# Attention row maxima read 512 keys at a time through four one-bank slots, with the attention stage written out group by group

## The chip, the core and the metric

The kernel runs on one core of one Trainium2 chip. The metric is the device time of one execution in microseconds (us). The kernel before takes 3453.68 us (median of 3 runs, 3448.55 to 3458.07).

## The reference, cut to what matters

Eight sequences of 1024 rows with 512 features go through a layer normalisation, an attention with 16 heads of 32 features (queries and keys come from low-rank projections and partly carry a rotary embedding), a residual sum, a second normalisation and a gated feed-forward part. The change touches only the attention:

```python
query = qt_c + qt_r
key = kt_c + kt_r
attn = jnp.einsum('bhqd,bhkd->bhqk', query, key) / scale
attn = jax.nn.softmax(attn, axis=-1)
out = jnp.einsum('bhqk,bhkd->bhqd', attn, value)
```

The softmax needs, for each of the 1024 queries of each head, the largest of its 1024 products with the keys.

## The kernel before, in words

The program has four stages, one behind the other: fold_block combines the projection weights, project_block normalises x and computes queries, keys and values, attend_block is the attention, and mix_block is everything behind it. The projection and the mixing stage are loops of the engines (Fori) with their first and last pieces written out.

The attention works on 32 groups (NG), each of one sequence and four heads. For one group PE computes two things:

- **The maxima of the group that comes next** (max_product, L242 to L261). A tile is 128 queries of one head against all 1024 keys. It takes two products of 512 keys each (the two values of kc), which go into the two banks of one slot. There are 2 slots of 2 banks (ps_m, MR = 2). VectorE (DVE) reads a whole slot, 1024 columns, with one reduce_max (max_reduce, L264 to L276), and writes one column of row_max. 16 tiles make a half of a group (HALF_TILES), and a group has two halves. Behind each half PE transposes the 16 columns of row_max in one of the same slots (L253), DVE turns the sign (L272, neg_max), and a transfer puts the result into one row of the query stack (stack_max, L279 to L284). PE may write a slot when DVE has read it (semaphore m_read, L249).
- **The attention of this group** (scores L797 to L806, pv L808 to L819, sums L821 to L831). A group has 8 rounds (UNITS). A round is 8 score products (512 queries against 128 keys of one head, the maximum subtracted through the extra row of the stacks), 8 exponentials on ScalarE (ACT, L893) out of a ring of three banks (ps_s), 16 narrow products that sum probabilities times values into ps_o (L818), and on GpSimd (POOL) one sum of the probabilities in pairs (L912; one more, L916, per half). Twice per group, 24 narrow products (L829) sum the pairs.

The order on PE is a hand-written table. SPREAD says how many steps of the maxima go ahead of each score product: one ahead of each of the 8 of a round. So a round on PE alternates maximum product, score product, eight times, and then come the 16 narrow products of the round before. Two places differ. In the fifth round two steps go ahead of the third score; the first of the two is the transpose for half 0. And the last step of a group, behind the narrow products of its eighth round, is the transpose for half 1. STEPS is 66 per group: 64 products and 2 transposes. Group 0 has a table of its own, SPREAD_FIRST, with nothing in its first two rounds and 11 steps in most of the others. The maxima of group 0 itself are computed in the last part of project_block, 5 or 6 steps for each projection item, in the PSUM tensors ps_turned and ps_rotated; DVE's part of it is at L641 to L652.

The attention stage is run through rounds(eng, step) (L735): groups 0 to 2 written out, then an engine loop over i = 1 to 9 with three groups in its body (27 groups), then groups 30 and 31 written out. In the loop, PE, DVE and the others take the values they wait for from registers. Names used below: "maximum product" is L258, "score product" L805, "the narrow products" L818.

Of the kernel before, what the change touches and what calls it, by code (L numbers as in the profile page):

```python
# [31 lines left out]
HG = P // HD  # L32
NG = B * FC
CH = 512
# [8 lines left out]
def is_first(c):  # L43

    return type(c) is int and c == 0


def fold_block(nc, sem, t, w, att, drams, load_x):
# [3 lines left out]
    with ExitStack() as ctx:  # L52
# [153 lines left out]
R3 = 3  # L206
NQ = S // CH
QT = CH // P
ROWS = 3 * HD
MR = 2  # L210
HALF_TILES = HG * QT


USE = ([(0, j) for j in range(HALF_TILES)] + [(1, 0), (0, HALF_TILES)] +
       [(1, j) for j in range(1, HALF_TILES + 1)])
USES = len(USE)
ROWS_AT = [USE.index((half, HALF_TILES)) for half in range(2)]
LAST_TILE_AT = [USE.index((half, HALF_TILES - 1)) for half in range(2)]
STEP = [(u, kc) for u, (half, j) in enumerate(USE) for kc in range(1 if j == HALF_TILES else S // CH)]
STEPS = len(STEP)  # L220
LOADS = 3 * NQ + 3


# [16 lines left out]
    sp.dma_start(att["v"][r][:], v_d[n]).then_inc(att["v_loaded"][r], 16)  # L240


def max_product(nc, pe, att, slots, ident, m, r, loads, step):


    u, kc = STEP[step]
    half, j = USE[u]
    slot = slots[u % MR]
    if kc == 0 and (u >= MR or not is_first(m)):  # L249
        pe.wait_ge(att["m_read"], m * USES + u - MR + 1)  # L250
    if j == HALF_TILES:
        pe.wait_ge(att["m_read"], m * USES + LAST_TILE_AT[half] + 1)
        nc.tensor.transpose(slot[0:HALF_TILES, 0, 0:P], att["row_max"][:, half, :], ident[:]).then_inc(att["m_scored"], 1)  # L253
        return
    if step == 0:
        pe.wait_ge(att["loaded"][r], 16 * LOADS * loads)
    h, q = divmod(j, QT)
    product = nc.tensor.matmul(slot[:, kc, :], att["q"][r][0:ROWS, half, h, q * P:(q + 1) * P],  # L258
                               att["k"][r][0:ROWS, h, kc * CH:(kc + 1) * CH], start=True, stop=True)
    if kc == S // CH - 1:  # L260
        product.then_inc(att["m_scored"], 1)  # L261


def max_reduce(nc, dve, att, slots, m, u):  # L264

    half, j = USE[u]
    slot = slots[u % MR]
    dve.wait_ge(att["m_scored"], m * USES + u + 1)
    if j == HALF_TILES:
        if not is_first(m):  # L270
            dve.wait_ge(att["m_stacked"][half], 16 * m)
        nc.vector.tensor_scalar(att["neg_max"][:, half, :], slot[0:HALF_TILES, 0, 0:P], -1.0, None,  # L272
                                ALU.mult).then_inc(att["m_read"], 1)
        return
    nc.vector.reduce_max(att["row_max"][:, half, j:j + 1], slot[:, :, :].rearrange("p k t -> p (k t)"),  # L275
                         AX).then_inc(att["m_read"], 1)  # L276


def stack_max(sp, held, att, n, r, half):  # L279
# [7 lines left out]
def project_block(nc, sem, held, t, w, x_v, x_in, x_loaded, att, grouped, scratch):  # L287
# [18 lines left out]
    with ExitStack() as ctx:  # L306
# [18 lines left out]
        rotated_too = ctx.enter_context(nc.psum_tensor("ps_rotated", [P, 2, CH], F32))  # L325
        ps_t = [turned[:, i, :] for i in range(TR)]
        ps_r = rotated_too[:, 0, :]
        ps_m = [turned, rotated_too]
        ps_p = [ctx.enter_context(nc.psum_tensor(f"ps_p{i}", [P, CH], F32)) for i in range(RING)]

        ln_step = sem("ln_step")
# [229 lines left out]
        def _(dve):  # L561
# [67 lines left out]
            def body(i, last):  # L629
                for par in range(CPB):  # L630
                    c = i * CPB + par
                    more = not (last and par == CPB - 1)
                    dve.wait_ge(rot_y, c + 1)
                    if not is_first(c):
                        dve.wait_ge(rot_sum, c * 2)
                    dve.sem_inc(held, 1)
                    nc.vector.stream_shuffle(y_swap[:, :], y_rot[:, :], SWAP).then_inc(rot_swap, 1)  # L637
                    if more:
                        norm(c + 1, 1 - par, i + 1 + par)
                    if last and par == CPB - 1:  # L640

                        for n in range(NI):
                            begun = ENDS[n - 1] if n else 0
                            uses = [u for u, kc in STEP[begun:ENDS[n]] if USE[u][1] == HALF_TILES or kc == 1]
# [22 lines left out]
def attend_block(nc, sem, held, t, att, scratch, o_d, l_d):  # L667
# [6 lines left out]
    UNITS = NQ * ROUNDS  # L674
    UT = KB * HG
    TILES = UNITS * UT
    SR = 3
    PR = 3
# [4 lines left out]
    RUN = TILES + NQ  # L683
    L_AT = UT
    HALF_RUN = ROUNDS * UT + 1
    assert RUN % SR == 0 and R3 * UNITS % PR == 0 and USES % MR == 0

    def is_last(n):
        return type(n) is int and n == NG - 1
# [15 lines left out]
    with ExitStack() as ctx:  # L705
# [9 lines left out]
        o_sb = sb("o_sb", [P, NQ, CH])  # L715
        l_sb = sb("l_sb", [P, NQ, CH])
        ps_s = [ctx.enter_context(nc.psum_tensor(f"ps_s{i}", [P, CH], F32)) for i in range(SR)]
        ps_m = [ctx.enter_context(nc.psum_tensor(f"ps_m{i}", [P, S // CH, CH], F32)) for i in range(MR)]
        ps_o = ctx.enter_context(nc.psum_tensor("ps_o", [P, CH], F32))

        rows_set = sem("rows_set")
# [10 lines left out]
        LOOPS = NG // R3  # L732
        REST = NG - LOOPS * R3

        def rounds(eng, step):  # L735

            for r in range(R3):
                step(0, r, r)
            with eng.Fori(1, LOOPS) as i:
                for r in range(R3):  # L740
                    step(i, r, i * R3 + r)
            for r in range(REST):
                step(LOOPS, r, LOOPS * R3 + r)

        @block.sync
        def _(sp):
            def store_o(n, qc):
                sp.wait_ge(o_out, n * NQ + qc + 1)
                sp.sem_inc(held, 1)
                sp.dma_start(o_d[n, :, qc * CH:(qc + 1) * CH], o_sb[:, qc, :]).then_inc(o_stored[qc], 16)  # L750

            def store_l(n, qc):
                sp.wait_ge(exped, taken(n, l_place(n, qc)))
                sp.sem_inc(held, 1)
                sp.dma_start(l_d[n, :, qc * CH:(qc + 1) * CH], l_sb[0:P - HD + 1:HD, qc, :]).then_inc(l_stored[qc], 16)

            def step(i, r, n):
# [19 lines left out]
            rounds(sp, step)  # L777
# [16 lines left out]
        def _(pe):  # L794
# [64 lines left out]
                    sums(n, 1)  # L859

            pe.wait_ge(att["ones_done"], 1)
            rounds(pe, step)

        @block.scalar
        def _(act):
# [30 lines left out]
                    take_o(n, 1)  # L896
                    take_l(n, 1)

            rounds(act, step)

        @block.gpsimd
        def _(pool):
# [16 lines left out]
            rounds(pool, step)  # L919

        @block.vector
        def _(dve):
            def step(i, r, n):
                if not is_last(n):
                    for u in range(USES):
                        max_reduce(nc, dve, att, ps_m, n + 1, u)

            rounds(dve, step)


def mix_block(nc, sem, held, t, x_d, o_d, l_d, inv_d, wo_d, wr_d, wk_d, wv_d, bo_d, mur_d, muk_d, out_d):
# [455 lines left out]
def block_program(nc, x, wdqT, bdq, wuq, buq, wqr, bqr, wkr, bkr, wdkvT, bdkv, wuk, buk, wuv, buv, wo, bo,  # L1387
# [10 lines left out]
    with ExitStack() as ctx:  # L1398
        def sem(name):
            return ctx.enter_context(nc.semaphore(name))  # L1400
# [8 lines left out]
        def keep(name, shape, dt=F32):  # L1409
            return kept.enter_context(nc.sbuf_tensor(name, shape, dt))  # L1410
# [2 lines left out]
            "q": [], "k": [], "v": [],  # L1413
            "ones": keep("ones", [P, HD]),
            "ones_done": sem("ones_done"),
            "row_max": keep("row_max", [P, 2, HG * QT]),
# [4 lines left out]
            "m_read": sem("m_read"),  # L1421
            "m_stacked": [sem(f"m_stacked{h}") for h in range(2)],
        }
        group_buffers(att, keep, 0)
# [73 lines left out]
```

## Time and profile before

| what | value |
|---|---|
| median of 3 runs | 3453.68 us (3448.55 to 3458.07) |
| the profiled execution's own time | 3445.66 us |
| its span, first to last instruction | 3443.9 us |
| PE busy | 3220.4 us, 94% |
| DVE busy | 2139.1 us, 62% |
| ACT busy | 1539.5 us, 45% |
| POOL busy | 2029.1 us, 59% |
| mean granted clock of PE | 0.975 |

The profile is of one execution. Busy shares are means over four stages that have different limits. The attention stage lies between about 686 and 2583 us of the span. PE's busy share counts matmuls whose ends are modelled and which overlap; how PE moves is read better from the starts in the timeline. A wait named "issue" is one for which the profile shows no releaser.

### The profile page before, as it was taken

To read this page: it belongs to the slowest core of one execution; us is meant where nothing else is said; L and a number is where in the kernel's file an instruction comes from. 1 tells how busy PE (TensorE), PEld (TensorE's weight loads), DVE (VectorE), ACT (ScalarE), POOL (GpSimd) and SP (SyncE) were. 2 spreads that over 40 slices of the span, in tenths; PEclk is the share of its full clock that TensorE was granted. 3 is DMA by queue.
4 is the path that set the end of the run, shared out by engine and by line. 5 is a ranking of instruction groups with operands and counts; after the bars stand their busy time and mean duration, and the time that the engine had idled before them with its cause. 6 is when DMAs were issued, how large, how long until landed. Compare 5 with 4: busy or idle time off the path is not lost. (4 is left out here: it accounts for less than half of the span.)

```text
span 3443.9 us, 49569 instructions
## 1 busy us (share of the span) xinstructions
PE 3220.4 (94%) x16020; PEld 2032.6 (59%) x16020; DVE 2139.1 (62%) x2249; ACT 1539.5 (45%) x2714; POOL 2029.1 (59%) x654
## 2 busy tenths in 40 slices
PE   7999999989999999999999999999995999999998
PEld 4888888744444444444444444444434777777777
DVE  4445545756666666666666666666617777777774
ACT  1212212156665666565666665666652322232232
POOL 0112112057777777777777777777773656556653
PEclk9999999989999999999999999999996999999999
DMA  3554545453232324242323223232205133233220
GB/s 103 176 170 160 183 167 174 141 109 79 68 82 57 93 51 96 54 96 54 88 62 77 73 67 82 57 90 53 53 13 173 50 98 97 60 86 97 81 65 37
DMA packets 179891, 316.27 MB, mean 92 GB/s; under 512 B 16081, under 2 KB 52081, under 8 KB 179697
## 3 DMA queue, kind: packets, MB, share of 16 engines
q1 hardware_dynamic: 179696, 313.70, 33.0%
q8 instruction: 120, 1.97, 0.2%
q14 instruction: 75, 0.61, 0.1%
HBM read 194.59 MB, written 118.49 MB: 91 GB/s over the span
## 5 line engine op out<-in xcount | busy, mean ns | idle before, releaser
L275 DVE TENSOR_REDUCE row_max<-ps_m 128x1 f32<-128x1024 f32 x992 | 1156.6, 1221 | 631.2 <-PE ps_m L258 630.6
L912 POOL TENSOR_TENSOR pairs<-probs 128x2048 f32<-128x2048 f32 x256 | 1167.9, 4574 | 477.2 <-ACT probs L893 477.2
L893 ACT ACTIVATE probs<-ps_s 128x512 f32<-128x512 f32 x2048 | 1085.9, 599 | 536.6 <-PE ps_s L805 520.3
L258 PE MATMUL ps_m<-k_stack,q_stack 96*128 96x512 f32 x1984 | 868.6, 439 | 97.3 <-DVE row_max L275 46.2
L805 PE MATMUL ps_s<-q_stack,k_stack 97*128 97x512 f32 x2048 | 823.4, 405 | 6.2 <-PEq L306 4.1
L258 PEld LDWEIGHTS ps_m<-k_stack,q_stack 96*128 96x128 f32 x1984 | 378.5, 191 | 532.8 <-DVE row_max L275 391.7
L818 PE MATMUL ps_o<-probs,v_tiles 128*32 128x512 f32 x4096 | 495.7, 602 | 0.0
L805 PEld LDWEIGHTS ps_s<-q_stack,k_stack 97*128 97x128 f32 x2048 | 394.7, 193 | 87.6 <-ACT probs L893 21.7
L541 POOL TENSOR_TENSOR y_cos<-y_rot,cos 64x512 f32<-64x512 f32 x16 | 20.6, 1284 | 472.8 <-DVE y_swap L637 472.8
L916 POOL TENSOR_TENSOR pairs<-pairs 128x2048 f32<-128x2048 f32 x64 | 293.2, 4581 | 5.0
L818 PEld LDWEIGHTS ps_o<-probs,v_tiles 128*32 128x32 f32 x4096 | 107.4, 109 | 248.6 <-issue 191.3
L1273 POOL TENSOR_TENSOR gate<-gate,xs 128x512 f32<-128x512 f32 x64 | 113.1, 1770 | 117.0 <-DVE gate L1363 117.0
L829 PE MATMUL ps_s<-pairs,ones 128*32 128x512 f32 x1536 | 177.6, 595 | 3.0 <-POOL pairs L912 3.0
L1091 PE MATMUL mix_p<-mix_w_o_hi,o_hi 128*128 128x512 f32 x256 | 110.8, 433 | 73.3 <-DVE gate L1363 34.9
L1195 ACT ACTIVATE relu<-mix_p 128x512 f32<-128x512 f32 x64 | 38.3, 598 | 308.1 <-PE mix_p L1093 253.1
L1352 DVE TENSOR_TENSOR ka_lo<-relu,ka_hi 128x512 fp32r<-128x512 f32 x64 | 117.3, 1833 | 49.0 <-ACT ka_hi L1189 46.7
L1244 POOL TENSOR_TENSOR xs<-mix_x_in,bo 128x512 f32<-128x512 f32 x64 | 114.7, 1796 | 25.6 <-DMA mix_x_in<-in_x 21.2
L829 PEld LDWEIGHTS ps_s<-pairs,ones 128*32 128x32 f32 x1536 | 49.8, 110 | 118.6 <-issue 113.8
L1331 DVE SCALAR_TENSOR_TENSOR mixed<-diff,mu_k,xT 128x512 f32<-128x512 f32 x64 | 111.4, 1799 | 0.6
L1092 PE MATMUL mix_p<-mix_w_o_lo,o_hi 128*128 128x512 f32 x256 | 109.4, 427 | 0.0
L1262 POOL TENSOR_TENSOR relu<-relu 128x512 f32<-128x512 f32 x64 | 68.8, 1084 | 68.8 <-ACT relu L1195 67.5
L1093 PE MATMUL mix_p<-mix_w_o_hi,o_lo 128*128 128x512 f32 x256 | 109.1, 426 | 0.0
(174 smaller groups left out, 4679.1 us busy)
## 6 DMA issues: line engine op xcount, KB each, us to landing
q_stack<-q_hi_scratch SPq DMA_DIRECT2D x128, 256.0 KB, 6.1
k_stack<-k_hi_scratch SPq DMA_DIRECT2D x64, 512.0 KB, 10.8
x_in<-in_x SPq DMA_DIRECT2D x16, 1024.0 KB, 5.7
q_hi_scratch<-st_hi SPq DMA_DIRECT2D x64, 256.0 KB, 2.3
q_lo_scratch<-st_lo SPq DMA_DIRECT2D x64, 256.0 KB, 2.6
k_hi_scratch<-st_hi SPq DMA_DIRECT2D x64, 256.0 KB, 2.4
k_lo_scratch<-st_lo SPq DMA_DIRECT2D x64, 256.0 KB, 2.7
v_scratch<-st_v SPq DMA_DIRECT2D x64, 256.0 KB, 2.3
```

The costliest lines, as they stand in the source:

```text
L258: product = nc.tensor.matmul(slot[:, kc, :], att["q"][r][0:ROWS, half, h, q * P:(q + 1) * P], att["k"][r][0:ROWS, h, kc * CH:(kc + 1) * CH ...
L275: nc.vector.reduce_max(att["row_max"][:, half, j:j + 1], slot[:, :, :].rearrange("p k t -> p (k t)"), AX).then_inc(att["m_read"], 1)
L805: nc.tensor.matmul(ps_s[v % SR][:, :], ks[r][:, a, kt * P:(kt + 1) * P], qs[r][:, qc, a, :], start=True, stop=True).then_inc(scored, 1)
L818: m = nc.tensor.matmul(ps_o[a * HD:(a + 1) * HD, :], vt[r][:, kt, a * HD:(a + 1) * HD], probs[:, (r * UNITS + u) % PR, k, a, :], start=kt ...
L829: m = nc.tensor.matmul(ps_s[v % SR][a * HD:(a + 1) * HD, :], ones[:, :], pairs[:, w, a, :], start=k == 0, stop=k == SUMS - 1)
L893: nc.scalar.activation(probs[:, (r * UNITS + u) % PR, x // HG, x % HG, :], ps_s[place(u * UT + x) % SR][:, :], ACT.Exp, scale=SCALE).then_ ...
L912: nc.gpsimd.tensor_tensor(pairs[:, w, :, :], probs[:, (r * UNITS + u) % PR, 0, :, :], probs[:, (r * UNITS + u) % PR, 1, :, :], ALU.add).th ...
L916: nc.gpsimd.tensor_tensor(pairs[:, 1, :, :], pairs[:, 0, :, :], pairs[:, 1, :, :], ALU.add).then_inc(pair_done, 1)
L1244: nc.gpsimd.tensor_tensor(xs[par][:, s, :], x_in[:, s, :], bo[:, :], ALU.add).then_inc(xb_done, 1)
L1273: nc.gpsimd.tensor_tensor(gate[:, s, :], gate[:, s, :], xs[par][:, s, :], ALU.add).then_inc(out_done, 1)
L1331: v = nc.vector.scalar_tensor_tensor(mixed[:, f, :], diff[:, f, :], mu_k[:, f:f + 1], prev[:, f, :], ALU.mult, ALU.add)
L1352: nc.vector.tensor_tensor(ka_lo[:, g, :], relu[:, g % RELU, :], ka_hi[:, g, :], ALU.subtract).then_inc(kal_done, 1)
```

## The change

- A slot is now one bank, and there are four (MR = 4; ps_m is four tensors of [128, 512], in project_block the four banks of ps_turned and ps_rotated).
- Each product of 512 keys is a use of its own: PE waits for its bank ahead of each product and signals behind each, and DVE reads each with a reduce_max of 512 columns. The result goes into part_max, two columns per tile.
- Behind the last reduction of a half, DVE waits for its own reads and takes the maximum of the two halves of part_max, 128 x 16, into row_max (new semaphore m_rows). The transpose waits for that.
- The transposes do not count in the rotation of the banks (BANK): a transpose uses the bank of the product that follows it, and that product waits until the transpose has been read (EARLIER).
- rounds() writes out all 32 groups; there is no engine loop in the attention stage, and all values that are waited for are constants.

The number of products, scores, exponentials, additions and transfers stays. DVE's reductions per group go from 32 of 1024 columns to 64 of 512, and 2 small maxima are added.

```diff
-MR = 2
+MR = 4
...
+def tiles(half, first, last):
+    return [(half, j, kc) for j in range(first, last) for kc in range(KCS)]
+
+
+USE = tiles(0, 0, HALF_TILES) + tiles(1, 0, 1) + [(0, HALF_TILES, 0)] + tiles(1, 1, HALF_TILES) + [(1, HALF_TILES, 0)]
 USES = len(USE)
...
+BANK = [sum(j < HALF_TILES for _, j, _ in USE[:u]) % MR for u in range(USES)]
+EARLIER = [max(v for v in range(-USES, u) if BANK[v] == BANK[u]) for u in range(USES)]
...
-    if kc == 0 and (u >= MR or not is_first(m)):
-        pe.wait_ge(att["m_read"], m * USES + u - MR + 1)
+    half, j, kc = USE[u]
+    bank = banks[BANK[u]]
+    if EARLIER[u] >= 0 or not is_first(m):
+        pe.wait_ge(att["m_read"], m * USES + EARLIER[u] + 1)
     if j == HALF_TILES:
-        pe.wait_ge(att["m_read"], m * USES + LAST_TILE_AT[half] + 1)
+        pe.wait_ge(att["m_rows"], m * 2 + half + 1)
...
-    nc.vector.reduce_max(att["row_max"][:, half, j:j + 1], slot[:, :, :].rearrange("p k t -> p (k t)"),
-                         AX).then_inc(att["m_read"], 1)
+    nc.vector.reduce_max(part_max[:, half, kc, j:j + 1], bank[:, :], AX).then_inc(att["m_read"], 1)
+    if j == HALF_TILES - 1 and kc == KCS - 1:
+        dve.wait_ge(att["m_read"], m * USES + u + 1)
+        nc.vector.tensor_tensor(row_max[:, half, :], part_max[:, half, 0, :], part_max[:, half, 1, :],
+                                ALU.max).then_inc(att["m_rows"], 1)
...
-        ps_m = [ctx.enter_context(nc.psum_tensor(f"ps_m{i}", [P, S // CH, CH], F32)) for i in range(MR)]
+        ps_m = [ctx.enter_context(nc.psum_tensor(f"ps_m{i}", [P, CH], F32)) for i in range(MR)]
...
-        def rounds(eng, step):
-
-            for r in range(R3):
-                step(0, r, r)
-            with eng.Fori(1, LOOPS) as i:
-                for r in range(R3):
-                    step(i, r, i * R3 + r)
-            for r in range(REST):
-                step(LOOPS, r, LOOPS * R3 + r)
+        def rounds(step):
+
+            for n in range(NG):
+                step(n // R3, n % R3, n)
```

The order on PE in the fifth round of a group, with what each instruction waits for, is this before (ident,row_max is the transpose for half 0):

```order
1350 L258 MATMUL ps_m<-k_stack,q_stack 128x512 [waits m_read]
1351 L805 MATMUL ps_s<-q_stack,k_stack 128x512 [waits exped,m_stacked1]
1352 L258 MATMUL ps_m<-k_stack,q_stack 128x512
1353 L805 MATMUL ps_s<-q_stack,k_stack 128x512 [waits exped]
1354 L253 MATMUL ps_m<-ident,row_max 16x128 [waits m_read]
1355 L258 MATMUL ps_m<-k_stack,q_stack 128x512 [waits m_read]
1356 L805 MATMUL ps_s<-q_stack,k_stack 128x512 [waits exped]
1357 L258 MATMUL ps_m<-k_stack,q_stack 128x512
```

and this with the change, at the same place:

```order
1325 L264 MATMUL ps_m<-k_stack,q_stack 128x512 [waits m_read]
1326 L805 MATMUL ps_s<-q_stack,k_stack 128x512 [waits exped,m_stacked1]
1327 L264 MATMUL ps_m<-k_stack,q_stack 128x512 [waits m_read]
1328 L805 MATMUL ps_s<-q_stack,k_stack 128x512 [waits exped]
1329 L259 MATMUL ps_m<-ident,row_max 16x128 [waits m_rows,m_read]
1330 L264 MATMUL ps_m<-k_stack,q_stack 128x512 [waits m_read]
1331 L805 MATMUL ps_s<-q_stack,k_stack 128x512 [waits exped]
1332 L264 MATMUL ps_m<-k_stack,q_stack 128x512 [waits m_read]
```

No instruction has changed its place on PE; every maximum product now has a wait for m_read, where every second one had it, and the transpose also waits for m_rows.

On DVE, one group's maxima before, in the part that was written out already:

```order
270 L275 TENSOR_REDUCE row_max<-ps_m 128x1 [waits m_scored] x17
271 L272 TENSOR_SCALAR neg_max<-ps_m 16x128 [waits m_stacked0,m_scored]
272 L275 TENSOR_REDUCE row_max<-ps_m 128x1 [waits m_scored] x15
273 L272 TENSOR_SCALAR neg_max<-ps_m 16x128 [waits m_stacked1,m_scored]
274 L275 TENSOR_REDUCE row_max<-ps_m 128x1 [waits m_scored] x17
```

and with the change:

```order
280 L280 TENSOR_REDUCE part_max<-ps_m 128x1 [waits m_scored] x32
281 L283 TENSOR_TENSOR row_max<-part_max 128x16 [waits m_read]
282 L280 TENSOR_REDUCE part_max<-ps_m 128x1 [waits m_scored] x2
283 L277 TENSOR_SCALAR neg_max<-ps_m 16x128 [waits m_stacked0,m_scored]
284 L280 TENSOR_REDUCE part_max<-ps_m 128x1 [waits m_scored] x30
285 L283 TENSOR_TENSOR row_max<-part_max 128x16 [waits m_read]
286 L277 TENSOR_SCALAR neg_max<-ps_m 16x128 [waits m_stacked1,m_scored]
```

The reductions are twice as many, and a small maximum of part_max stands behind the 32nd and the 64th of them.

## Rows read from the trace of the kernel before

**Rows 1.** Stretches of one group: length, busy (x) PE PEld DVE ACT POOL, PEclk, DMA

```profile
817.30:874.90 57.60, 55.43 (x312) 27.36 (x308) 37.74 (x34) 36.24 (x68) 45.62 (x11) 1.00 0.31 74
...
1224.30:1286.00 61.70, 56.88 (x312) 28.70 (x308) 38.00 (x34) 36.57 (x68) 45.65 (x11) 0.97 0.30 70
```

**Rows 2.** Timeline of PE, one round: start us, us, engine line op

```profile
1509.53 0.50 PE L258 MATMUL ps_m<-k_stack,q_stack 96*128 96x512 f32 x1
1509.87 0.40 PE L805 MATMUL ps_s<-q_stack,k_stack 97*128 97x512 f32 x1
...
1511.27 0.39 PE L805 MATMUL ps_s<-q_stack,k_stack 97*128 97x512 f32 x1
1511.82 0.50 PE L258 MATMUL ps_m<-k_stack,q_stack 96*128 96x512 f32 x1 [0.15 <-DVE row_max L275]
1512.16 0.39 PE L805 MATMUL ps_s<-q_stack,k_stack 97*128 97x512 f32 x1
...
1512.95 0.50 PE L258 MATMUL ps_m<-k_stack,q_stack 96*128 96x512 f32 x1
...
1513.75 0.39 PE L805 MATMUL ps_s<-q_stack,k_stack 97*128 97x512 f32 x1
1514.07 1.92 PE L818 MATMUL ps_o<-probs,v_tiles 128*32 128x512 f32 x16
1515.92 0.50 PE L258 MATMUL ps_m<-k_stack,q_stack 96*128 96x512 f32 x1
```

**Rows 3.** Timeline of DVE in the same round

```profile
1510.54 4.64 DVE L275 TENSOR_REDUCE row_max<-ps_m 128x1 f32<-128x1024 f32 x4 [1.76 <-PE ps_m L258]
```

**Rows 4.** Timeline of DVE in the projection: operations on 512 columns back to back

```profile
672.95 0.68 DVE L614 TENSOR_TENSOR st_v<-ps_p,bv 128x512 f32<-128x512 f32 x1
673.55 1.22 DVE L275 TENSOR_REDUCE row_max<-ps_rotated 128x1 f32<-128x1024 f32 x1
```

**Rows 5.** Lines of DVE by form: busy us, mean ns | idle before

```profile
L272 DVE TENSOR_SCALAR neg_max<-ps_m 16x128 fp32r<-16x128 f32 x62 | 17.0, 274 | 32.9 <-PE ps_m L253 32.9
...
L1308 DVE BATCH_NORM_AGGREGATE mix_mv<-mix_stats 128x2 f32<-128x6 f32 x64 | 6.1, 158 | 2.4 <-DVE mix_stats L1303 2.0
...
L203 DVE TENSOR_TENSOR bk<-bk,bkr 128x3 f32<-128x3 f32 x1 | 0.2, 163 | 0.0
```

**Rows 6.** Timelines of PE and DVE, transpose for half 0

```profile
1551.61 0.28 PE L253 MATMUL ps_m<-ident,row_max 128*16 128x128 f32 x1
1552.85 0.50 PE L258 MATMUL ps_m<-k_stack,q_stack 96*128 96x512 f32 x1 [0.96 <-DVE row_max L275]
...
1552.71 0.27 DVE L272 TENSOR_SCALAR neg_max<-ps_m 16x128 fp32r<-16x128 f32 x1
```

**Rows 7.** Timeline of PE, transposes for half 1, one group apart

```profile
1522.33 0.28 PE L253 MATMUL ps_m<-ident,row_max 128*16 128x128 f32 x1
1522.36 0.47 PE L258 MATMUL ps_m<-k_stack,q_stack 96*128 96x512 f32 x1
...
1579.89 0.28 PE L253 MATMUL ps_m<-ident,row_max 128*16 128x128 f32 x1
1583.34 0.50 PE L258 MATMUL ps_m<-k_stack,q_stack 96*128 96x512 f32 x1 [3.17 <-issue]
```

**Rows 8.** Timeline of PE, transposes for half 1 of the first and last loop trips

```profile
1047.56 0.28 PE L253 MATMUL ps_m<-ident,row_max 128*16 128x128 f32 x1
...
2462.84 0.28 PE L253 MATMUL ps_m<-ident,row_max 128*16 128x128 f32 x1
```

**Rows 9.** Waits of PE from 700 to 2570 us: total us, times, longest

```profile
PE ps_m L258 <- issue: 23.3, 8, 3.2
```

**Rows 10.** Timeline of PE, group 0, one round with 11 steps

```profile
716.18 0.73 PE L258 MATMUL ps_m<-k_stack,q_stack 96*128 96x512 f32 x2
...
724.17 0.50 PE L258 MATMUL ps_m<-k_stack,q_stack 96*128 96x512 f32 x1
```

**Rows 11.** Stretch of the last projection part, columns as in the first group

```profile
640.00:655.00 15.00, 15.00 (x66) 12.15 (x65) 13.72 (x15) 2.62 (x4) 0.00 (x0) 1.00 0.32 120
```

More of the change, by code:

```diff
@@ L209 @@
 ROWS = 3 * HD
-MR = 2
+MR = 4
 HALF_TILES = HG * QT
-USE = ([(0, j) for j in range(HALF_TILES)] + [(1, 0), (0, HALF_TILES)] +
-       [(1, j) for j in range(1, HALF_TILES + 1)])
+KCS = S // CH
+def tiles(half, first, last):
+    return [(half, j, kc) for j in range(first, last) for kc in range(KCS)]
+USE = tiles(0, 0, HALF_TILES) + tiles(1, 0, 1) + [(0, HALF_TILES, 0)] + tiles(1, 1, HALF_TILES) + [(1, HALF_TILES, 0)]
 USES = len(USE)
[L217 to L220, printed above, removed]
+STEPS = USES
+ROWS_AT = [USE.index((half, HALF_TILES, 0)) for half in range(2)]
+BANK = [sum(j < HALF_TILES for _, j, _ in USE[:u]) % MR for u in range(USES)]
+EARLIER = [max(v for v in range(-USES, u) if BANK[v] == BANK[u]) for u in range(USES)]
 LOADS = 3 * NQ + 3
@@ L240, in load_group, with max_product, max_reduce @@
     sp.dma_start(att["v"][r][:], v_d[n]).then_inc(att["v_loaded"][r], 16)
[L243 to L248, printed above, removed]
-    if kc == 0 and (u >= MR or not is_first(m)):
-        pe.wait_ge(att["m_read"], m * USES + u - MR + 1)
+def max_product(nc, pe, att, banks, ident, m, r, loads, u):
+    half, j, kc = USE[u]
+    bank = banks[BANK[u]]
+    if EARLIER[u] >= 0 or not is_first(m):
+        pe.wait_ge(att["m_read"], m * USES + EARLIER[u] + 1)
     if j == HALF_TILES:
-        pe.wait_ge(att["m_read"], m * USES + LAST_TILE_AT[half] + 1)
-        nc.tensor.transpose(slot[0:HALF_TILES, 0, 0:P], att["row_max"][:, half, :], ident[:]).then_inc(att["m_scored"], 1)
+        pe.wait_ge(att["m_rows"], m * 2 + half + 1)
+        nc.tensor.transpose(bank[0:HALF_TILES, 0:P], att["row_max"][:, half, :], ident[:]).then_inc(att["m_scored"], 1)
         return
-    if step == 0:
+    if u == 0:
         pe.wait_ge(att["loaded"][r], 16 * LOADS * loads)
     h, q = divmod(j, QT)
[L258 to L267, printed above, removed]
+    nc.tensor.matmul(bank[:, :], att["q"][r][0:ROWS, half, h, q * P:(q + 1) * P],
+                     att["k"][r][0:ROWS, h, kc * CH:(kc + 1) * CH], start=True, stop=True).then_inc(att["m_scored"], 1)
+def max_reduce(nc, dve, att, banks, m, u):
+    half, j, kc = USE[u]
+    bank = banks[BANK[u]]
+    part_max, row_max, neg_max = att["part_max"], att["row_max"], att["neg_max"]
     dve.wait_ge(att["m_scored"], m * USES + u + 1)
@@ L271, in max_reduce @@
             dve.wait_ge(att["m_stacked"][half], 16 * m)
-        nc.vector.tensor_scalar(att["neg_max"][:, half, :], slot[0:HALF_TILES, 0, 0:P], -1.0, None,
+        nc.vector.tensor_scalar(neg_max[:, half, :], bank[0:HALF_TILES, 0:P], -1.0, None,
                                 ALU.mult).then_inc(att["m_read"], 1)
         return
-    nc.vector.reduce_max(att["row_max"][:, half, j:j + 1], slot[:, :, :].rearrange("p k t -> p (k t)"),
-                         AX).then_inc(att["m_read"], 1)
+    nc.vector.reduce_max(part_max[:, half, kc, j:j + 1], bank[:, :], AX).then_inc(att["m_read"], 1)
[3 more added lines that the diff above has]
+                                ALU.max).then_inc(att["m_rows"], 1)
 def stack_max(sp, held, att, n, r, half):
@@ L327, in project_block @@
         ps_r = rotated_too[:, 0, :]
-        ps_m = [turned, rotated_too]
+        ps_m = [two[:, i, :] for two in (turned, rotated_too) for i in range(2)]
         ps_p = [ctx.enter_context(nc.psum_tensor(f"ps_p{i}", [P, CH], F32)) for i in range(RING)]
@@ L643, in body @@
                             begun = ENDS[n - 1] if n else 0
-                            uses = [u for u, kc in STEP[begun:ENDS[n]] if USE[u][1] == HALF_TILES or kc == 1]
+                            uses = range(begun, ENDS[n])
                             max_reduce(nc, dve, att, ps_m, 0, uses[0])
@@ L685, in attend_block @@
     HALF_RUN = ROUNDS * UT + 1
-    assert RUN % SR == 0 and R3 * UNITS % PR == 0 and USES % MR == 0
+    assert RUN % SR == 0 and R3 * UNITS % PR == 0
     def is_last(n):
@@ L730, in attend_block @@
         block = ctx.enter_context(nc.Block())
-        LOOPS = NG // R3
-        REST = NG - LOOPS * R3
-        def rounds(eng, step):
-            for r in range(R3):
-                step(0, r, r)
-            with eng.Fori(1, LOOPS) as i:
-                for r in range(R3):
-                    step(i, r, i * R3 + r)
-            for r in range(REST):
-                step(LOOPS, r, LOOPS * R3 + r)
+        def rounds(step):
+            for n in range(NG):
+                step(n // R3, n % R3, n)
         @block.sync
@@ L776, in _ @@
                              ks[0][ROWS:ROWS + 1, :, :].bitcast(F32)).then_inc(rows_set, 16)
-            rounds(sp, step)
+            rounds(step)
             store_o(NG - 1, 1)
@@ L861, in _ @@
             pe.wait_ge(att["ones_done"], 1)
-            rounds(pe, step)
+            rounds(step)
         @block.scalar
@@ L897, in step @@
                     take_l(n, 1)
-            rounds(act, step)
+            rounds(step)
         @block.gpsimd
@@ L917, in step @@
                                                 ALU.add).then_inc(pair_done, 1)
-            rounds(pool, step)
+            rounds(step)
         @block.vector
@@ L926, in step @@
                         max_reduce(nc, dve, att, ps_m, n + 1, u)
-            rounds(dve, step)
+            rounds(step)
 def mix_block(nc, sem, held, t, x_d, o_d, l_d, inv_d, wo_d, wr_d, wk_d, wv_d, bo_d, mur_d, muk_d, out_d):
@@ L1415, in block_program @@
             "ones_done": sem("ones_done"),
+            "part_max": keep("part_max", [P, 2, KCS, HG * QT]),
             "row_max": keep("row_max", [P, 2, HG * QT]),
@@ L1421, in block_program @@
             "m_read": sem("m_read"),
+            "m_rows": sem("m_rows"),
             "m_stacked": [sem(f"m_stacked{h}") for h in range(2)],
```

## The prediction

> **What bounds the kernel now.** I looked first at stretches of one group each in the attention stage. A group takes 57.60 us, of which DVE is busy 37.74, ACT 36.24, POOL 45.62, and PE 55.43 at full granted clock [rows 1]. So none of the other three engines is full, and PE is the one to follow. The first group of a loop trip is longer, 61.70 us, at a mean clock of 0.97 [rows 1].
>
> Next, the timeline of one round on PE [rows 2]. From the first score product (1509.87) to the fourth (1511.27) it makes six steps in 1.40 us, 0.233 each: this is PE's own pace. The first product behind a break takes 0.34 us to the next one (1509.53 to 1509.87). Twice PE loses this pace, and both times a maximum product waits for its slot: 1511.27 to 1511.82 is 0.55 instead of 0.23, and then 0.34 instead of 0.23, together 0.43 us; from 1512.16 to 1512.95, three steps take 0.79 instead of 0.70, and again 0.11 behind it, together 0.20. That is 0.6 us in a round of 6.39 us (1509.53 to 1515.92). DVE, which it waits for, idles 1.76 us before its four reductions of 4.64 us [rows 3]. So DVE is not too slow; the slots are too coarse. PE must wait until 1024 columns have been read before it may write 512.
>
> Last, the ends of the groups: the transpose for half 1 is followed by a product 0.03 us later inside a trip (1522.33, 1522.36) and 3.45 us later at the end of a trip (1579.89, 1583.34), with "issue" as the reason [rows 7].
>
> **Part 1: slots of one bank.** DVE's spacing of reductions of 1024 columns is (4.64 - 1.22) / 3 = 1.14 us [rows 3, 4]. For 512 columns: the 128-column operation out of PSUM takes 0.27 us and the 1024-column one 1.22, which is 1.06 ns a column [rows 4, 5], so 512 fewer columns save 0.54 and leave a spacing of 0.60 and a duration of 0.68. Another operation on 512 columns out of PSUM shows just that: 0.68 us long, and the next begins 0.60 behind it [rows 4]. I take 0.60.
>
> Now a round by hand, from its first maximum product at 0. With PE's own pace the eight maximum products begin at 0, 0.57, 1.04, 1.51, 1.98, 2.44, 2.91 and 3.38, the last score product at 3.61, the narrow products at 3.93 (0.32 behind it, 1513.75 to 1514.07) and the next round at 5.78 (1.85 more) [rows 2]. A reduction begins 0.43 us behind the start of its product (product 0.23 behind 1509.87, reduction at 1510.54), 0.54 behind the first [rows 2, 3]. So the reductions begin at 0.54, 1.14, 1.74 and so on to 4.74, and the last ends at 5.42. A bank is free 0.06 us behind the end of its reduction (1510.54 + 1.22, then 1511.82) [rows 2 to 4]. The eighth product needs the fourth reduction (2.34 + 0.68 + 0.06 = 3.08), and its weights are loaded from 3.15 on: in time, by 0.07 us. The others have more room. So no wait is left within a round: 5.78 in place of 6.39, **-0.60 us, eight times a group, -4.8**. Per group DVE is then busy 64 x 0.60 = 38.4 us by spacing, where 32 x 1.14 = 36.5 stood.
>
> **Part 2: the transposes.** For half 0 PE waited 1.24 us from the transpose to the next product (1551.61 to 1552.85), because that one's slot was still being read [rows 6]. Now the next product shares the bank with the transpose, and DVE reads the transpose behind two reductions: the transpose goes at 1.04, the second reduction begins at 1.14, the sign change at 1.74, ends at 2.01, and the product starts at 2.07: 1.03, so -0.2.
>
> For half 1 a wait is added. The last reduction ends at 5.42; then DVE waits for its own write, 0.15 us (2.4 us in 16 such places), and takes the maximum, 0.16 us by a small operation of the same kind [rows 5]. That is 5.73, and with 0.06 5.79: the transpose goes at its old place, or 0.05 later. But the product behind it, the first of the next group, now waits for the sign change: 0.31 us until DVE begins, 0.27, 0.06, together 0.65 where 0.03 stood [rows 5, 7]. **+0.65.** Behind this product all of PE's next group is queued, so the whole of it counts. The same small maximum for half 0 runs while PE does narrow products, and costs nothing; without that cover it would cost the same 0.3.
>
> Per group: -4.8 - 0.2 + 0.65 = -4.35. For the 30 groups 1 to 30: **-130 us**. Group 31 has no maxima.
>
> **Part 3: group 0 and the projection.** A round of group 0 with 11 steps takes 7.99 us [rows 10]. At PE's pace it is 19 steps, some 6.5 us; DVE needs 11 x 0.60 = 6.6, and PE can go on while up to four banks are full. I take 7.0 for each of six rounds: -6 us. In the last projection part DVE is busy 13.72 of 15 us, PE all 15 [rows 11]. A pair of reductions takes 1.20 in place of 1.14, 32 pairs: 2 us more work for DVE, which had 1.3 us in 15 to spare, and finer slots for PE. I put it at 0, between -1 and +3.
>
> **Part 4: no engine loop.** Between the transposes for half 1 of the first and the last trip lie 24 groups and 8 jumps back: 1415.28 us [rows 8], where 24 groups of 57.56 (1522.33 to 1579.89) make 1381.4 [rows 7]. The jumps cost 33.8 us, 4.2 each: 3.2 of wait [rows 9], and the rest from the granted clock, 0.97 on average over that group [rows 1]: a stretch at the lower level (1.2 GHz), after PE had stood still. Group 2 is written out already, and runs in 57.60 us at clock 1.00, as groups in the loop do [rows 1, 7]; so instructions in a straight line arrive in time. **-33.8 us.** The Trainium skill, Advanced Engine Details and Errata, section Control Flow Timing, gives some 108 ns for a compare and branch; by it the eight jumps would give back 0.9 us and not 33.8. The trace does not agree, and it decides.
>
> POOL is the next that could bind: ten operations, 45.62 us of a group that becomes 53.2 [rows 1]. It keeps 7 us; ACT, at 36.24, keeps 17.
>
> **The sum**: -130 - 6 + 0 - 34 = -170. From the profiled execution's own 3445.66 us: 3276. This execution was 8 us faster than the median of its kernel's runs, 3453.68, and 3 faster than the fastest; from the median the same sum gives 3284. I forecast 3280.
>
> **The rivals.**
>
> *A: DVE holds PE within the burst.* The eighth product has only 0.07 us of room. If a reduction doesn't overlap with the one before, its spacing is its whole duration, 0.68. The fourth reduction then begins at 2.58, its bank is free at 3.32, and the weights wait 0.17 us; the last reduction ends 0.56 later than in my table, and both transposes slip with it (0.14 for half 0, 0.5 for half 1). I make that between +0.3 and +1.2 us a group, by how much of the 0.17 is hidden behind the score product ahead: 30 times, +9 to +36, so 3289 to 3316, in the middle 3302. For it: in the new kernel each reduction has its own product to wait for. Against it: the spacing of 1.14 also holds a wait for each reduction [rows 3], and 0.60 is seen on 512 columns [rows 4]. The Trainium skill, VectorE: DVE Perf Modes, section on the TRN2 errata, speaks against the change: many small tiles pay a fixed cost each, 120 cycles out of PSUM, so 632 cycles at 0.96 GHz, an estimate of 0.66 us for 512 columns; by that page it would be this rival. The trace's spacings are shorter, by 0.06.
>
> *B: the jumps' time stays*, as a wait for instructions now spread over the straight code: 3280 + 34 = 3314. Against it stands group 2 [rows 1].
>
> *C: slower.* DVE's reductions become serial through their semaphores: each 0.68 and then 0.15 for its own write, as where DVE waits for itself [rows 5], 0.83 us. Eight of them are 6.64 a round, over the 6.39 of now, and DVE is the bound; with the transposes behind it, some +3 us a group over now, 30 times 3 less the 34 of the loop: 3500. It decides from a spacing of about 0.79, where the rounds lose what the loop gives. DVE's waits are on PE, not on itself, save two a group, so little speaks for it.
>
> **How the numbers follow.** Forecast 0.74, A 0.15, B 0.06, C 0.03, and 0.02 for gains that meet a bound I have not seen and come out even. The range takes in, below, -6 us for reductions that leave even the transposes less to wait for, -1 for the projection, and the scatter of the runs (5 either way) and the 4 us between the two bases; above, rival A up to its end of 3316. So 3264 to 3318; B lies in it too, at 3314; C and the even case do not. Within 0.3% (10 us, about what a measurement of this kernel can tell from no change) of 3453.68: 0.02. Faster 0.95, slower 0.03.
>
> **What would show it.** A group in the stage should take 53.2 us, all 30 alike, with PE's clock at 1.00 throughout; rounds of 5.8 us, with no wait of a maximum product for DVE but at the transposes, 1.0 us and 0.65 us a group; reductions 0.68 long and 0.60 apart; DVE busy some 44 us a group by durations; no "issue" wait of 3 us. Wrong: reductions 0.66 or more apart with waits at the eighth product (A), "issue" waits on PE in straight code (B), DVE without idle time (C), or narrow products of the pair sums that wait for POOL.

## The result, and the profile after

| | before | changed |
|---|---|---|
| median | 3452.77 us (4 runs, 3448.55 to 3458.07) | 3663.46 us (4 runs, 3635.48 to 3720.84) |
| ratio | 1 | 1.0582 (95%: 1.0521 to 1.0644) |
| mean granted clock of the profiled execution | 0.975 | 0.918 |

The change was to save 170 us, and it costs 211. The longest of the four runs, 3720.84 us, is a slow one, 2.3% above the fastest: the ratio leaves it out (the other three have a median of 3660.57 us, at clocks of 0.920 to 0.921). It is the execution that was profiled (span 3719.0 us), so the rows below are its, and they are set against other profiled executions, never against a median.

PE's granted clock in 40 slices of the span (9 is 90% of full speed or more), from the page of the kernel before:

```profile
PEclk9999999989999999999999999999996999999999
```

The same line of the changed kernel's page, and groups of its instructions (busy us, mean ns | idle before, releaser):

```profile
PEclk8999999889998989888888888898897899999999
...
L280 DVE TENSOR_REDUCE part_max<-ps_m 128x1 f32<-128x512 f32 x1984 | 1238.0, 682 | 497.8 <-PE ps_m L264 497.2
L912 POOL TENSOR_TENSOR pairs<-probs 128x2048 f32<-128x2048 f32 x256 | 1163.4, 4556 | 753.5 <-ACT probs L893 753.4
L283 DVE TENSOR_TENSOR row_max<-part_max 128x16 f32<-128x16 f32 x64 | 337.9, 5280 | 2.2
```

The reductions are as forecast (682 ns), and the attention stage, slices 8 to 30, has lost clock. The small maximum by itself, with its minimum, median and maximum in ns, and the waits of PE in groups 1 to 30 (total us, times, longest):

```profile
L283 DVE TENSOR_TENSOR row_max<-part_max x64: 174/6248/6293, 659.6 to 2782.4; 128x16 f32<-128x16 f32 x64
```

```profile
PE ps_m L259 <- DVE row_max L283: 283.2, 61, 6.0
PE ps_m L264 <- DVE neg_max L277: 39.0, 60, 0.9
```

This is the operation that the prediction priced at 0.16 us. Two of its 64 do last 0.17: those for group 0, in the projection stage, where POOL does nothing. In the attention stage 50 last 6.2 to 6.3 us, 10 last 1.7 to 1.8 (all ten are of half 1), and 2 last 3.7. The transpose on PE waits for each, and behind the transpose stands everything that PE has to do. Here is one, first on DVE, then on POOL, then on PE (start us, us, engine, line and operation):

```profile
1576.47 4.87 DVE L280 TENSOR_REDUCE part_max<-ps_m 128x1 f32<-128x512 f32 x8 [0.92 <-PE ps_m L264]
1581.38 6.28 DVE L283 TENSOR_TENSOR row_max<-part_max 128x16 f32<-128x16 f32 x1
1587.58 1.27 DVE L280 TENSOR_REDUCE part_max<-ps_m 128x1 f32<-128x512 f32 x2
```

```profile
1578.58 9.05 POOL L912 TENSOR_TENSOR pairs<-probs 128x2048 f32<-128x2048 f32 x2
```

```profile
1570.14 0.50 PE L264 MATMUL ps_m<-k_stack,q_stack 96*128 96x512 f32 x1
...
1575.94 0.50 PE L264 MATMUL ps_m<-k_stack,q_stack 96*128 96x512 f32 x1
...
1582.53 0.39 PE L805 MATMUL ps_s<-q_stack,k_stack 97*128 97x512 f32 x1
1587.81 0.37 PE L259 MATMUL ps_m<-ident,row_max 128*16 128x128 f32 x1 [4.88 <-DVE row_max L283]
1589.10 0.79 PE L264 MATMUL ps_m<-k_stack,q_stack 96*128 96x512 f32 x1 [0.93 <-DVE neg_max L277]
1589.70 0.63 PE L805 MATMUL ps_s<-q_stack,k_stack 97*128 97x512 f32 x1
```

The maximum begins 2.80 us into a POOL operation and ends at 1587.66, just behind the second one (1578.58 + 9.05 = 1587.63). Its end follows POOL's, not its own work: all 62 in the attention stage end 0.03 to 0.04 us behind the end of a POOL operation. PE's round is 5.80 us (1570.14 to 1575.94), as forecast. Then PE stands still for 4.88 us, and a score product behind that shows 0.63 us where it showed 0.39: the granted clock is 0.50 from 1589.1 to 1592.0, the lower level of 1.2 GHz, and was 1.00 from 1581.7 to 1582.9.

Stretches, columns as in [rows 1]: the group with this wait, and groups 1 to 30 together.

```profile
1553.90:1623.20 69.30, 57.18 (x307) 31.30 (x306) 52.85 (x68) 35.63 (x68) 49.64 (x11) 0.88 0.26 61
...
759.20:2788.90 2029.70, 1711.11 (x9181) 946.52 (x9182) 1540.79 (x2040) 1068.04 (x2040) 1363.13 (x300) 0.89 0.26 61
```

A group takes 67.66 us on average (2029.7 / 30), where 53.2 was forecast. In the profile of before the clue stood in lines that the prediction passed over. Three of DVE's lines, by form:

```profile
L1352 DVE TENSOR_TENSOR ka_lo<-relu,ka_hi 128x512 fp32r<-128x512 f32 x64 | 117.3, 1833 | 49.0 <-ACT ka_hi L1189 46.7
...
L1363 DVE TENSOR_TENSOR gate<-mix_p,gate 128x512 f32<-128x512 f32 x64 | 39.9, 678 | 18.0 <-PE mix_p L1093 18.0
...
L606 DVE TENSOR_TENSOR st_lo<-group,st_hi 128x512 fp32r<-128x512 f32 x32 | 21.9, 687 | 1.3
```

All three are the same kind of instruction, with two inputs and 512 columns. L606 reads both from SBUF where POOL is idle, and lasts 0.69 us. L1363 takes one input out of PSUM; 45 of its 64 stand beside a POOL operation, and none lasts over 0.70. L1352 reads both from SBUF in the mixing stage, where POOL works, and lasts 1.83 on average: the 17 that no POOL operation overlaps take 0.68 to 0.69, the other 47 take 1.12 to 5.03.

### The profile page after: what moved, and what is told of

It is laid out like the page before. It is cut to its first block and busy times, and to the rows that moved or that the text cites. A ratio compares the mean times of both kernels' runs of the same rounds, so it can differ in the third digit from the quotient of the medians.

```text
span 3719.0 us, 43839 instructions
## 1 busy us (share of the span) xinstructions
PE 3265.4 (88%) x16020; PEld 2151.4 (58%) x16020; DVE 2549.8 (69%) x3337; ACT 1518.9 (41%) x2714; POOL 2029.5 (55%) x654
## 5 line engine op out<-in xcount | busy, mean ns | idle before, releaser
L280 DVE TENSOR_REDUCE part_max<-ps_m 128x1 f32<-128x512 f32 x1984 | 1238.0, 682 | 497.8 <-PE ps_m L264 497.2
L912 POOL TENSOR_TENSOR pairs<-probs 128x2048 f32<-128x2048 f32 x256 | 1163.4, 4556 | 753.5 <-ACT probs L893 753.4
L893 ACT ACTIVATE probs<-ps_s 128x512 f32<-128x512 f32 x2048 | 1065.3, 618 | 820.6 <-PE ps_s L805 810.8
L264 PE MATMUL ps_m<-k_stack,q_stack 96*128 96x512 f32 x1984 | 892.7, 451 | 45.4 <-DVE neg_max L277 39.8
L805 PE MATMUL ps_s<-q_stack,k_stack 97*128 97x512 f32 x2048 | 888.9, 437 | 5.8 <-PEq L314 4.0
L264 PEld LDWEIGHTS ps_m<-k_stack,q_stack 96*128 96x128 f32 x1984 | 422.2, 213 | 328.5 <-DVE part_max L280 136.9
L805 PEld LDWEIGHTS ps_s<-q_stack,k_stack 97*128 97x128 f32 x2048 | 435.1, 213 | 150.8 <-ACT probs L893 19.5
L818 PE MATMUL ps_o<-probs,v_tiles 128*32 128x512 f32 x4096 | 513.6, 621 | 0.0
L283 DVE TENSOR_TENSOR row_max<-part_max 128x16 f32<-128x16 f32 x64 | 337.9, 5280 | 2.2
L916 POOL TENSOR_TENSOR pairs<-pairs 128x2048 f32<-128x2048 f32 x64 | 293.0, 4578 | 5.0
L259 PE MATMUL ps_m<-ident,row_max 128*16 128x128 f32 x62 | 21.8, 352 | 283.4 <-DVE row_max L283 283.4
L1352 DVE TENSOR_TENSOR ka_lo<-relu,ka_hi 128x512 fp32r<-128x512 f32 x64 | 108.8, 1699 | 48.9 <-ACT ka_hi L1189 46.7
L622 DVE TENSOR_TENSOR st_v<-ps_p,bv 128x512 f32<-128x512 f32 x64 | 44.2, 691 | 98.1 <-PE ps_p L451 98.1
```

The costliest lines, as they stand in the source:

```text
L264: nc.tensor.matmul(bank[:, :], att["q"][r][0:ROWS, half, h, q * P:(q + 1) * P], att["k"][r][0:ROWS, h, kc * CH:(kc + 1) * CH], start=True, ...
L280: nc.vector.reduce_max(part_max[:, half, kc, j:j + 1], bank[:, :], AX).then_inc(att["m_read"], 1)
L283: nc.vector.tensor_tensor(row_max[:, half, :], part_max[:, half, 0, :], part_max[:, half, 1, :], ALU.max).then_inc(att["m_rows"], 1)
L805: nc.tensor.matmul(ps_s[v % SR][:, :], ks[r][:, a, kt * P:(kt + 1) * P], qs[r][:, qc, a, :], start=True, stop=True).then_inc(scored, 1)
L818: m = nc.tensor.matmul(ps_o[a * HD:(a + 1) * HD, :], vt[r][:, kt, a * HD:(a + 1) * HD], probs[:, (r * UNITS + u) % PR, k, a, :], start=kt ...
L893: nc.scalar.activation(probs[:, (r * UNITS + u) % PR, x // HG, x % HG, :], ps_s[place(u * UT + x) % SR][:, :], ACT.Exp, scale=SCALE).then_ ...
```

## The experiments

Theory L: a DVE operation with two SBUF inputs does not get at the memory while POOL works, so the small maximum lasts until POOL stops. Theory S: the finer slots, or the straight code, are what costs. In the expectations L is called the port theory; their wait theory is a third one, that the 6 us are DVE's wait for its own write, or its reading of what it has just written.

**One input instead of two.** The same maximum from the same bytes, as a reduction.

```diff
-        nc.vector.tensor_tensor(row_max[:, half, :], part_max[:, half, 0, :], part_max[:, half, 1, :],
-                                ALU.max).then_inc(att["m_rows"], 1)
+        nc.vector.reduce_max(row_max[:, half, :], part_max[:, half, :, :].rearrange("p k j -> p j k"),
+                             AX).then_inc(att["m_rows"], 1)
```

> The changed kernel, but the small maximum of part_max (L283) is a reduce_max with one input in SBUF in place of a tensor_tensor with two. Port theory (an operation of DVE with two inputs in SBUF does not start while POOL runs, and POOL's next operation can go first): the small maximum takes 0.15 to 0.3 us everywhere, PE's wait for it at the transposes (283 us) goes, the granted clock stays at 1.00 in the stage, a group takes 53 to 53.5 us, and the kernel 3270 to 3290 us. Wait theory (DVE's wait for its own write, or reading just what it wrote, is what takes 6 us): the small maximum stays at 1.7 or 6.2 us and the kernel at 3640 to 3680 us.

Measured: 3284.09 us (4 runs, 3281.36 to 3285.74), ratio to before 0.9512 (0.9496 to 0.9528). The small maximum, its place on PE, and the stretches of groups 1 to 30 and of one group:

```profile
L283 DVE TENSOR_REDUCE row_max<-part_max x64: 186/188/192, 660.6 to 2356.4; 128x16 f32<-128x32 f32 x64
```

```profile
1450.20 0.28 PE L259 MATMUL ps_m<-ident,row_max 128*16 128x128 f32 x1
1450.85 0.50 PE L264 MATMUL ps_m<-k_stack,q_stack 96*128 96x512 f32 x1 [0.37 <-DVE neg_max L277]
```

```profile
756.90:2356.80 1599.90, 1566.41 (x9181) 856.65 (x9181) 1198.33 (x2040) 1039.63 (x2040) 1366.47 (x300) 1.00 0.33 78
1450.30:1503.60 53.30, 52.18 (x307) 28.55 (x306) 39.94 (x68) 34.66 (x68) 45.65 (x11) 1.00 0.34 81
```

One instruction kind turns 3663 into 3284, with POOL's load unchanged. Theory S falls, and the wait theory too, for the reduction waits for the same write and reads the same bytes. Against this kernel the loss of the changed one in groups 1 to 30 can be divided: 2029.70 - 1599.90 = 429.8 us. PE's busy time is 1711.11 - 1566.41 = 144.7 us longer for the same instructions, at a clock of 0.89 instead of 1.00; the other 285.1 is idle time, of which PE's row of waits for L283 has 283.2. So in this execution a third of the loss is the clock's, behind the standstills. From the median of the other three, 3660.57, to 3284.09 it is 376 us, and no row shows how that divides.

**Two inputs, but little for POOL to do.** POOL's sums cover 128 of 2048 columns, L912 in the same way as L916. The rest of the sums is left out, so the result is not the reference's; POOL fills the whole of pairs with ones once, at its start.

```diff
-nc.gpsimd.tensor_tensor(pairs[:, 1, :, :], pairs[:, 0, :, :], pairs[:, 1, :, :],
+nc.gpsimd.tensor_tensor(pairs[:, 1, :, 0:32], pairs[:, 0, :, 0:32], pairs[:, 1, :, 0:32],
```

> The changed kernel with the two-input maximum kept, but POOL's pair sums (L912, L916) cover 128 of 2048 columns; the rest of the sums of the probabilities is left out. Port theory: POOL's operations take some 0.3 to 0.5 us, so the small maximum is 0.17 us nearly everywhere and never over 1 us; the kernel takes 3260 to 3290 us. Wait theory: the small maximum stays at 1.7 to 6.2 us, and the kernel over 3600 us.

Measured: 3278.64 us (1 run). The small maximum and a group:

```profile
L283 DVE TENSOR_TENSOR row_max<-part_max x64: 174/175/178, 660.4 to 2355.5; 128x16 f32<-128x16 f32 x64
```

```profile
1449.00:1502.30 53.30, 52.18 (x314) 28.55 (x306) 39.90 (x69) 34.65 (x68) 4.53 (x11) 1.00 0.34 81
```

The same instruction as in the changed kernel, in the same place, takes 0.175 us once POOL is busy 4.53 us of a group instead of 45.65. So it takes both: two inputs from SBUF on DVE, and work on POOL. Without one of them the 6 us are gone, and the kernel's time with them.

**The kernel before with such a maximum added.** Behind the last reduction of each half, a maximum of constants that nothing needs.

```diff
+    if j == HALF_TILES - 1:
+        nc.vector.tensor_tensor(att["spare"][:, 0:HALF_TILES], att["ones"][:, 0:HALF_TILES],
+                                att["ones"][:, HALF_TILES:2 * HALF_TILES], ALU.max)
```

> The kernel before, with one added maximum of 128 x 16 with two inputs in SBUF (constants) behind the last reduction of each half, for which nobody waits, and ahead of which DVE waits for nothing. Port theory: it takes up to 6.3 us where POOL runs, DVE's next reduction and the sign change are held behind it, PE waits for slots, and the kernel gets 150 to 350 us slower. Wait theory: 0.17 us each, and the kernel within 10 us of before.

Measured: 3752.82 us (1 run) against 3450.14, so +303.

```profile
L278 DVE TENSOR_TENSOR spare<-ones x64: 165/5253/5353, 659.7 to 2826.6; 128x16 f32<-128x16 f32 x64
```

With coarse slots and the loop, the same few bytes cost the same kind of time, though nobody waits for the result: DVE's next reductions stand behind it, and PE's slots stay full. The constants were written long before, and DVE waits for nothing ahead of it. So the cost is neither the slots' nor the straight code's, nor that of reading what was just written.

**The kernel before, only written out.** rounds() of the changed kernel in the kernel before, in which a step's number is still n:

```diff
-            with eng.Fori(1, LOOPS) as i:
-                for r in range(R3):
-                    step(i, r, i * R3 + r)
...
+            for n in range(NG):
+                step(n // R3, n % R3, n)
```

> The kernel before, with its attention stage written out and nothing else. Theory that the jumps back cost 34 us (8 of 4.2 us): the waits of 3 us named issue are gone, all groups take 57.6 us, and the kernel is 30 to 38 us faster than before, about 3419 us. Rival (the time stays, as waits for code in the straight part): within 5 us of before.

Measured: 3418.29 us (4 runs, 3414.4 to 3419.17), ratio 0.99 (0.9883 to 0.9916), so -32 us. PE's waits in the stage:

```profile
PE ps_m L258 <- DVE row_max L275: 44.5, 120, 1.0
PE ps_m L258 <- DMA k_stack<-k_lo_scratch: 4.9, 1, 4.9
```

There is no "issue" row any more, and groups 1 to 30 take 57.5 to 57.6 us each. From here to the one-input kernel it is 3418.3 - 3284.1 = 134 us: the slots' share.

**Four banks or finer reads?** The one-input kernel with MR = 2, so two one-bank slots:

```diff
-MR = 4
+MR = 2
```

> The one-input kernel with two banks in place of four: 512 keys read by themselves, but only two slots. If the gain of the rounds comes from the four banks and not from the finer reading alone, PE must wait for the reduction of two products before: by the same table as in the prediction a round takes some 6.9 us, a group about 62 us, the kernel 3530 to 3570 us, slower than before. If the finer reading alone is enough, 53 to 54 us a group and 3285 to 3310 us.

Measured: 3577.32 us (1 run), just above the range, a group at 62.4. Waits of PE's weight loads for a bank, with two slots and then with four, in the one-input kernel:

```profile
PEld ps_m L264 <- DVE part_max L280: 526.4, 1429, 0.8
```

```profile
PEld ps_m L264 <- DVE part_max L280: 136.9, 180, 0.8
```

With two banks, reads of 512 columns lose 4.8 us a group to the kernel before (57.6), which has four banks in two slots; with four they win 4.3. So finer reads with half the banks lose, and what pays is the same four banks coming free one at a time, so that PE can be ahead by whole products. (Four slots inside the engine loop were not tried.)

**Two inputs for half 1 alone**, one input for half 0:

```diff
+        if half == 1:
+            nc.vector.tensor_tensor(row_max[:, half, :], part_max[:, half, 0, :], part_max[:, half, 1, :],
+                                    ALU.max).then_inc(att["m_rows"], 1)
+            return
```

> The changed kernel with two inputs for the small maximum of half 1 only, one input for half 0. The stall theory says that each of the two stops PE: half 1, whose transpose is the next thing on PE but two us, should carry half or more of the 376 us between the changed kernel and the one-input kernel: 3284 + 160 to 230 = 3445 to 3515 us. If the loss came from one place alone, it would be 3284 or 3660.

Measured: 3360.39 us (1 run), +76 over the one-input kernel, a miss, about half of the least that was expected. The maximum's row, and one of them on DVE and POOL:

```profile
L284 DVE TENSOR_TENSOR row_max<-part_max x32: 174/1775/6220, 684.5 to 2431.3; 128x16 f32<-128x16 f32 x32
```

```profile
1484.07 1.78 DVE L284 TENSOR_TENSOR row_max<-part_max 128x16 f32<-128x16 f32 x1
```

```profile
1481.26 9.03 POOL L916 TENSOR_TENSOR pairs<-probs 128x2048 f32<-128x2048 f32 x2
```

The maximum asks 2.81 us into POOL's operation, as in the stretch of the changed kernel above (2.80), but ends 1.78 later, between POOL's two operations (1481.26 + 4.52 = 1485.78; it ends at 1485.85). In groups 1 to 30, 28 of 30 got in there; in the changed kernel it was 10 of the 30 of half 1, and none of the 30 of half 0. The price falls from 6.3 to 1.8 us, and the time with it. So this run doesn't say how the loss of the changed kernel is shared between the two halves, and what decides at such a boundary is not settled.

**POOL's sums in four pieces.** The changed kernel, with each POOL operation of 2048 columns as four of 512 (L912 in the same way):

```diff
-nc.gpsimd.tensor_tensor(pairs[:, 1, :, :], pairs[:, 0, :, :], pairs[:, 1, :, :],
-                        ALU.add).then_inc(pair_done, 1)
+for a in range(HG):
+    p_ = nc.gpsimd.tensor_tensor(pairs[:, 1, a, :], pairs[:, 0, a, :], pairs[:, 1, a, :], ALU.add)
+p_.then_inc(pair_done, 1)
```

> The changed kernel with the two-input maximum kept, and each of POOL's sums over 2048 columns split into four over 512 columns (some 1.15 us each). If DVE's waiting operation gets in at the next end of an operation of POOL, the small maximum takes at most 1.4 us, and the kernel about 3290 to 3340 us. If POOL's next operation, where one stands ready, always goes first, the small maximum still lasts until POOL runs out of ready work: 1.7 to 6.5 us as now, and the kernel 3620 to 3700 us.

Measured: 3874.4 us (1 run), above what either theory gave.

```profile
L283 DVE TENSOR_TENSOR row_max<-part_max x64: 176/7922/7945, 659.3 to 2935.3; 128x16 f32<-128x16 f32 x64
```

```profile
1624.53 7.92 DVE L283 TENSOR_TENSOR row_max<-part_max 128x16 f32<-128x16 f32 x1
```

```profile
1622.57 9.84 POOL L913 TENSOR_TENSOR pairs<-probs 128x512 f32<-128x512 f32 x8
```

The maximum asks in the second of eight POOL operations, passes six boundaries, and ends at 1632.45, behind the last (1632.41). So do all 60 of groups 1 to 30. If it had only had to wait for the operation in progress, at most one of 9.84 / 8 = 1.23 us would have passed. So shorter pieces didn't help here: each time DVE waited until POOL had nothing ready. That was the second theory; its time was too low, since the maximum now asks 1.96 us into POOL's stretch, not 2.80, and the stretch is 9.84 us long, not 9.05.

**A version beyond both.** The one-input kernel, in which the transposes take a bank of their own turn, so that the product behind one needn't wait for its reading:

```diff
+def bank_of(banks, m, u):
+
+    return banks[(m * USES + u) % MR]
...
-    bank = banks[BANK[u]]
-    if EARLIER[u] >= 0 or not is_first(m):
-        pe.wait_ge(att["m_read"], m * USES + EARLIER[u] + 1)
+    bank = bank_of(banks, m, u)
+    if m * USES + u >= MR:
+        pe.wait_ge(att["m_read"], m * USES + u - MR + 1)
```

> The kernel with the one-input maximum, and in addition each transpose takes a bank of its own in the rotation, so the product behind it waits for the read of four uses before and not for the sign change. In the one-input run that product starts 1.0 us (half 0) and 0.65 us (half 1) behind the transpose. Theory (these two waits are all of PE's lost time that is left): a group goes from 53.33 to 51.4 to 51.7 us, the kernel to 3225 to 3240 us. Rival (DVE is then so full that it holds PE elsewhere in the burst): a group stays over 52.5 us, the kernel over 3255 us.

Measured: 3232.83 us (4 runs, 3230.35 to 3237.97), ratio to before 0.9376 (0.9357 to 0.9395), the fastest here. Groups take 51.7 us, and PE's wait for neg_max is gone from the rows of waits. Sharing the bank, a part of the change, cost 1.6 us a group.

## Why the prediction was wrong

It gave 3280 us and faster at 0.95; 3663 lies outside its range and on the other side. **One term failed: the small maximum of Part 2**, "0.16 us by a small operation of the same kind [rows 5]", and beside it, for half 0, "runs while PE does narrow products, and costs nothing". The row, L203, has the same operation and nearly the same size, but it runs where POOL has nothing to do. In the attention stage POOL is busy 45.62 of 57.60 us [rows 1], and there the 62 maxima last 5.44 us on average (5.28 over all 64). It was the price of an operation alone, taken to a place where it isn't alone. For half 0 the cover of 2 us of narrow products was too short for 6.3. The prediction named POOL only as an engine whose busy time might fill; it didn't ask what POOL's work does to DVE's. With no standstill in its sum it had nothing for the clock either, which made a third of the loss in the profiled execution.

The other steps, read in the one-input kernel, where only this term is repaired:

- **Rounds**, 5.78 forecast: 5.80 in the changed kernel itself. Duration 0.68 and spacing 0.60 forecast: 0.682, and (4.87 - 0.68) / 7 = 0.60. The room of 0.07 us at the eighth product was enough; rival A did not come.
- **Transpose for half 1**, 0.65 to the next product: 1450.20 to 1450.85, 0.65.
- **Transpose for half 0**, 1.03 to the next product: 1.02 (median of 31).
- **DVE's wait for its own write**, 0.15: 0.04 in the changed kernel (the reductions end at 1581.34, the maximum begins at 1581.38). It was read from another instruction, and too high by 0.1.
- **A group**, 53.2: 53.3, at clock 1.00. The slots' share, -130 and -6: -134.
- **DVE's busy time**, 44 us a group by durations: 64 reductions of 0.683 are 43.7. (The stretch shows 39.94, since it counts overlapping operations once.)
- **Group 0**, -6: 70.9 us between the transposes for half 1 around it, where the kernel before had 74.4 and the one only written out 76.3. So -3.5 or -5.4, from single executions: somewhat less than was put on it.
- **The projection**, between -1 and +3: the last transpose there stands at 685.9 instead of 685.3, +0.6.
- **No loop**, -33.8: -32. Rival B did not come. (Of a jump's 4.2 us the prediction called 3.2 wait; that is the longest of [rows 9], and the eight average 2.9. The sum went by the 4.2.)
- **The sum** from the median, 3284: 3284.09. That it meets to 0.1 us is luck: beside the runs of before made with it (3450.14), the gain is 166 us, where 170 was forecast.

Rival C had the sign but not the place: it foresaw reductions made serial by their semaphores, and put 3500 on it. DVE did become what PE waits for, through one operation per half and not through 64 reductions.

The Trainium skill, SBUF — State Buffer, section SBUF: two separate sides, has the rule that would have given the right sign: DVE and GpSimd share a pair of ports under an exclusive lock, DVE needs it for an operation with two SBUF inputs (against a GpSimd operation that reads SBUF, as POOL's sums do), it is held for the whole instruction, and "the other fully blocks". The runs agree that it blocks (0.17 us alone, 6.25 beside POOL) and that one input doesn't (0.188). They show waits, not ports, so that it is this lock is the skill's account and not a finding here. And the wait can be longer than one instruction, for the section doesn't say who goes next: had DVE got in when POOL's operation in progress ended, the maximum at 1581.38 would have ended at about 1583.1, and the one beside the quarters within 1.23 us. They passed one boundary and six.

## What to carry to other kernels

Before pricing an added operation from another stage's row, compare what the other engines do in the two places: a VectorE operation with two SBUF inputs, however small, may wait for all the work that GpSimd has ready, so give it one input (a reduction over both) or one from PSUM when it stands on the path. Cutting GpSimd's operations smaller didn't free it here. And a standstill of TensorE can be paid twice, once as a wait and again as clock.

## What had not been expected of the hardware

- DVE's two-input maximum of 128x16: 0.174 us with POOL idle; 1.7 to 6.3 us beside POOL operations of 4.5 us; 7.9 us beside eight of 1.23 us. Mostly POOL's next ready operation goes first: in 50 of 60 cases of the changed kernel, and in all 60 of the kernel before with the maximum added and of the one with quarters. Yet in 10 of the 30 of half 1, and in 28 of 30 where half 0 had one input, DVE got in between two, though it asked at the same point of the operation (2.8 us in). Why is open.
- PE's standstills, two in a group and 4.6 us each on average (283.2 / 61), go with a granted clock of 0.89 in the stage instead of 1.00, and PE's busy time there is 1711 us instead of 1566. With the standstills gone, the clock is back at 1.00 with the same instructions on PE.
- A reduction over two columns in place of a two-input maximum costs 0.014 us more by itself (188 against 174 ns).
